# A one-core decoder block on Trainium2: turns placed later among the MLP's matmuls, first rows' passes ahead of a turn, decay buffers apart, and the gate chain in another order

## What is computed

```python
x = x + attn(layernorm(x))        # a Mamba-2 mixer, then a gated MLP (width 1024)
x = x + xattn(layernorm(x), ctx)  # an mLSTM cell: q from x, k = v = ctx, 4 heads of 64
x = x + ffn(layernorm(x))         # FP4 quantised gate/up/down, width 704

# gates of the cell: i and f are linear in [q, k, v]
lf = log_sigmoid(f); cs = cumsum(lf)
log_D[s, t] = cs[s] - cs[t] + lf[t] + i[t]   for t <= s
m = rowmax(log_D); D = exp(log_D - m)
C = (q k^T / 8) * D
h = C / (max(|rowsum(C)|, exp(-m)) + 1e-8) @ v      # then a per-head norm
```

## Time and profile before

| | |
|---|---|
| median of 3 runs | 634.5 us (633.87 to 637.78) |
| the profiled execution | 634.09 us, of which 632.3 us are the profile's span |
| PE busy | 575.8 us, 91% |
| DVE busy | 446.1 us, 71% |
| ACT busy | 270.2 us, 43% |
| POOL busy | 145.6 us, 23% |
| mean granted TensorE clock | 0.959 of 2.4 GHz |

### The profile page before, as it was taken

The page is one execution under the profiler, slowest core; times in us unless marked ns, Lnnn a source line. Parts: engine busy times, 40 slices in busy tenths (PEclk is TensorE's granted clock), DMA queues, the critical chain, the costliest instruction groups (busy, mean ns, idle before and its releaser), DMA issues. The chain is left out here.

```text
span 632.3 us, 9628 instructions
## 1 busy us (share of the span) xinstructions
PE 575.8 (91%) x3023; PEld 467.0 (74%) x3023; DVE 446.1 (71%) x969; ACT 270.2 (43%) x563; POOL 145.6 (23%) x209
## 2 busy tenths in 40 slices
PE   7799998999999889899999999679975899999995
PEld 6576665788888778777888888668862577777774
DVE  5885898299896134444445456657898999999994
ACT  3566777776794421221111110155523344444431
POOL 4120000145543110111011010203575322222200
PEclk9899998799999989999999999799976899999998
DMA  8201001000000500000000000223400000000000
GB/s 296 91 18 33 17 13 55 4 23 6 6 4 2 202 2 1 1 1 1 0 1 1 1 1 0 68 71 110 142 17 1 1 10 16 17 17 17 17 18 25
DMA packets 22528, 20.99 MB, mean 33 GB/s; under 512 B 12120, under 2 KB 20696, under 8 KB 22104
## 3 DMA queue, kind: packets, MB, share of 16 engines
q1 hardware_dynamic: 22008, 20.41, 10.0%
q10 hardware_dynamic: 480, 0.07, 0.1%
HBM read 16.04 MB, written 2.34 MB: 29 GB/s over the span
## 5 line engine op out<-in xcount | busy, mean ns | idle before, releaser
L762 PE MATMUL ps<-xnT,w_fc 128*128 128x256 f32 x512 | 113.9, 383 | 0.0
L762 PEld LDWEIGHTS ps<-xnT,w_fc 128*128 128x128 f32 x512 | 97.5, 192 | 13.1
L1545 PE MATMUL ps<-w_fc,scores 128*128 128x352 f32 x256 | 83.0, 479 | 6.1 <-ACT scores L1611 6.1
L1545 PEld LDWEIGHTS ps<-w_fc,scores 128*128 128x128 f32 x256 | 49.1, 197 | 33.9 <-ACT scores L1611 8.2
L1165 DVE TENSOR_TENSOR xs<-ps,xs 128x512 f32<-128x512 f32 x32 | 22.1, 692 | 71.3 <-ACT xs L972 71.3
L972 ACT ACTIVATE xs<-ps 128x512 f32<-128x512 f32 x32 | 19.1, 597 | 104.9 <-PE ps L762 67.2
L775 PE MATMUL ps<-zs,xs 128*128 128x256 f32 x256 | 56.6, 379 | 0.0
L775 PEld LDWEIGHTS ps<-zs,xs 128*128 128x128 f32 x256 | 48.6, 190 | 6.6
L1060 DVE SCALAR_TENSOR_TENSOR fold<-xpad,conv_w,fold 128x256 f32<-128x256 f32 x120 | 50.6, 479 | 0.8
L1563 PE MATMUL ps<-u_res,hT 128*128 128x256 f32 x192 | 45.9, 391 | 3.8 <-DVE scores L1717 2.8
L1563 PEld LDWEIGHTS ps<-u_res,hT 128*128 128x128 f32 x192 | 37.4, 195 | 11.8 <-issue 3.0
(11 more groups left out here) (266 smaller groups left out, 1185.2 us busy)
## 6 DMA issues: line engine op xcount, KB each, us to landing
zs<-in_ffn_w SPq DMA_DIRECT2D x1, 2112.0 KB, 10.7
x_res<-in_x SPq DMA_DIRECT2D x8, 256.0 KB, 7.4
w_fc<-in_w_fc SPq DMA_DIRECT2D x1, 2048.0 KB, 10.3
xnT<-in_ctxT SPq DMA_DIRECT2D x8, 256.0 KB, 3.1
xs<-in_ctxT SPq DMA_DIRECT2D x8, 256.0 KB, 3.3
xs<-xnT SPq DMA_DIRECT2D x8, 256.0 KB, 3.4
xs<-in_ctx SPq DMA_DIRECT2D x16, 128.0 KB, 2.6
out<-scores SPq DMA_DIRECT2D x16, 128.0 KB, 1.7
```

Source lines behind the costliest of these rows:

```text
L762: last = pe.matmul(bank[half + r][:, i * S:(i + 1) * S], m.w_fc1[:, kk, col:col + P], m.xnT[:, b, kk * S:(kk + 1) * S], start=(kk == 0), s ...
L1545: last = pe.matmul(bank[1 + j][:, 0:HALF], xT[:, p, k * P:(k + 1) * P], m.w_gu[:, k, j * HALF:(j + 1) * HALF], start=(k == 0), stop=(k == ...
```

## The change

- **MLP** (steps 18 on): PE does `turn_xn(b-5)` after pair 2 of `fc1` instead of before it; ACT does `turned_xn` at the end of the same step instead of at the start of the next.
- **First rows**: in step 3, PE does both passes `rows(0, 0)` and `rows(0, 1)` before `turn_u(4)`, instead of after it and near the step's end.
- **Decay buffers apart**: `segs` keeps only `stationary` and `moving`; the working buffers lie in `e_own` and in the last batch's part of `xs`. `set_segs` goes; three DVE memsets (as 1024 float32 a partition each) stand at the very start, before `stats(0)`. SP waits for its own store of the rows. `rmax` lies in the `stationary` half of `segs` afterwards and is cleared by POOL in step 19 (`fills`), with the ones for the scan.
- **Gate chain**: `gate_rows` writes the gate values in the layout the chain wants, so the four copies go; `lf + i` is formed before the turn; the scan and the operation after it read PSUM itself; the parts of R come before `nm`. PE turns six weight groups first, then 4 `keep_warm` transposes instead of 26, then `lf`, then `lf + i`, then the other six groups; the last 10 `keep_warm` go. ACT stores the parts after all saves, then does the exp of `nm`. POOL sets only the ones column of `v`. ACT ends front with a small Exp.

```diff
@@ -208,6 +208,8 @@
...
         m.graw = sb("graw", [P, T, 2 * XH])
+        m.gates = sb("gates", [P, 2, C, B * XH])
+        m.run_ones = sb("run_ones", [B * XH, S])
         m.a_tok = sb("a_tok", [P, C * B * XH])
...
@@ -235,6 +237,8 @@
...
             m.scores = sb("scores", [P, B, 3 * P])
+            m.segs = sb("segs", [P, 2048])
+            m.rmax = m.segs[:, 0:1024].bitcast(BF16).rearrange("p (r t) -> p r t", r=2)
             m.dt = sb("dt", [P, T, NH])
...
@@ -433,19 +437,22 @@
     W = T * NH
-    segs = sb("segs", [P, 2048])
-    over_segs = carver(segs)
-    work = [over_segs(f"sp{k}", [P, W]) for k in range(5)]
-    raw = over_segs("dt_raw", [P, W])
-    ones = over_segs("ones", [P, P])
-    both = over_segs("cs", [P, 2, P])
-    rest = over_segs("cs_rest", [P, 2, P])
-    pieces = over_segs("cs_pieces", [P, 3 * P]).bitcast(BF16).rearrange("p (g k t) -> p g k t", g=2, k=3)
+    segs = m.segs
+    over_e = carver(e_own)
+    work = [over_e(f"sp{k}", [P, W]) for k in range(5)]
+    raw = over_e("dt_raw", [P, W])
+    ones = over_e("ones", [P, P])
+    over_last_x = carver(m.xs[:, T - C:, :].rearrange("p t e -> p (t e)"))
+    both = over_last_x("cs", [P, 2, P])
+    rest = over_last_x("cs_rest", [P, 2, P])
+    pieces = over_last_x("cs_pieces", [P, 3 * P]).bitcast(BF16).rearrange("p (g k t) -> p g k t", g=2, k=3)
     rows_dram = nc.dram_tensor("segment_rows", (W, 6, P), BF16).ap()
...
     ROWS_IN = 4 * 16
+    PAIR_OF_ONES = 1.0 + 0x3F80 * 2.0 ** -23
+    PAIR_OF_MINUS_ONES = -(1.0 + 0xBF80 * 2.0 ** -23)
     CTX_SUMS = B - 1
...
@@ -503,6 +510,7 @@
...
         sp.dma_start(rows_dram, pieces.rearrange("p g k t -> p (g k) t")).then_inc(s["seg_stored"], 16)
+        sp.wait_ge(s["seg_stored"], 16)
         sp.wait_ge(s["segs_set"], 1)
...
@@ -589,9 +597,17 @@
...
+        def fills():
+            pool.wait_ge(s["seg_ps"], 2 * T)
+            pool.memset(m.rmax, 0.0)
+            pool.memset(m.run_ones[:], 1.0).then_inc(s["filled"], 1)
+            pool.wait_ge(s["filled"], 2)
+
         for k in range(STEPS):
...
             on(rstds, 2 * k + 1)
+            if k == MLP + 1:
+                fills()
             if k == 4:
...
@@ -803,8 +819,12 @@
...
                 on(channels, k - 2, [0, 1, 2])
+                if k == 3:
+                    rows(0, 0)
+                    rows(0, 1)
                 on(turn_u, 2 * k - 2)
-                on(rows, k - 3, 0)
+                if k > 3:
+                    on(rows, k - 3, 0)
                 on(channels, k - 2, [3, 4])
...
@@ -812,7 +832,8 @@
...
                     sum_steps()
-                on(rows, k - 3, 1)
+                if k > 3:
+                    on(rows, k - 3, 1)
                 on(turn_x, k - 3, 1)
...
@@ -838,8 +859,11 @@
...
                 ctx_sums_last()
-            on(turn_xn, b - 5)
+            if k < MLP:
+                on(turn_xn, b - 5)
             on(fc1, k - MLP, 2)
+            if k >= MLP:
+                on(turn_xn, b - 5)
             on(fc1, k - MLP, 3)
...
@@ -979,7 +1003,8 @@
...
                 step_exp()
-            on(turned_xn, b - 6)
+            if k <= MLP:
+                on(turned_xn, b - 6)
             for i in range(3):
...
@@ -1011,11 +1036,18 @@
...
             on(silu_gate, k - MLP, 3)
+            if k >= MLP:
+                on(turned_xn, b - 5)
             on(turned_q, k - MLP - 2)
+        act.activation(ve[:, 0, :], m.minus_half[:, 0:C], ACT.Exp)
...
         dve.memset(xpad[:, :, :, 0:PAD], 0.0).then_inc(s["pads_clear"], 1)
+        dve.memset(segs[:, 0:1024], 0.0)
+        dve.memset(segs[:, 1024:2048], PAIR_OF_MINUS_ONES).then_inc(s["segs_kept"], 1)
+        dve.wait_ge(s["segs_kept"], 1)
+        dve.memset(segs[0:12, 0:1024], PAIR_OF_ONES).then_inc(s["segs_set"], 1)
...
@@ -1100,13 +1132,6 @@
...
-        def set_segs():
-            dve.wait_ge(s["seg_stored"], 16)
-            dve.memset(stationary, 0.0)
-            dve.memset(moving, -1.0).then_inc(s["segs_kept"], 1)
-            dve.wait_ge(s["segs_kept"], 1)
-            dve.memset(stationary[0:12, :, :], 1.0).then_inc(s["segs_set"], 1)
-
         def inputs(b):
...
@@ -1185,8 +1210,9 @@
...
             here = m.graw[:, C * b:C * (b + 1), :]
-            dve.tensor_tensor(here, bank[7][:, 0:C * 2 * XH].rearrange("p (c g) -> p c g", c=C),
-                              here, ALU.add).then_inc(g["gates_saved"], 1)
+            dve.tensor_tensor(m.gates[:, :, :, XH * b:XH * (b + 1)],
+                              bank[7][:, 0:C * 2 * XH].rearrange("p (c g h) -> p g c h", c=C, g=2),
+                              here.rearrange("p c (g h) -> p g c h", g=2), ALU.add).then_inc(g["gates_saved"], 1)
...
@@ -1219,8 +1245,6 @@
...
                 soft_rest()
-            if k == 8:
-                set_segs()
             on(convolve, k - 2, [2, 3])
...
@@ -1255,13 +1279,12 @@
...
     rest = sb("max_rest", [ROWS, 2, S])
-    ig = sb("ig", [P, C, ROWS])
-    fg = sb("fg", [P, C, ROWS])
+    ig, fg = (m.gates[:, k].rearrange("p c r -> p (c r)") for k in range(2))
+    shifted = sb("ig_lf", [P, C * ROWS])
     lf = sb("lf", [P, C * ROWS])
     work = [sb(f"lsp{k}", [P, C * ROWS]) for k in range(5)]
-    igT, lfT, cs, aT, R, nm = (sb(n, [ROWS, S]) for n in ("igT", "lfT", "cs", "aT", "R", "nm"))
-    ones = sb("ones", [ROWS, S])
-    s = m.plain("gt_dve gt_act gt_pe gt_ones w_turned w_saved")
+    cs, aT, R, nm = (sb(n, [ROWS, S]) for n in ("cs", "aT", "R", "nm"))
+    s = m.plain("gt_dve gt_act gt_pe gt_pad w_turned w_saved")
...
@@ -1277,26 +1300,21 @@
...
     BETWEEN = 6
-    by_chunk = lambda lo: m.graw[:, :, lo:lo + XH].rearrange("p (b c) h -> p c b h", c=C)
-    split = lambda t: t[:].rearrange("p c (b h) -> p c b h", h=XH)
     block = m.block
...
     def _(pool):
-        pool.memset(m.w_dn[FF - (KF - 1) * P:, KF - 1, :], 0.0).then_inc(s["gt_ones"], 1)
-        pool.wait_ge(s["gt_ones"], 1)
-        pool.memset(ones[:], 1.0).then_inc(s["gt_ones"], 1)
+        pool.memset(m.w_dn[FF - (KF - 1) * P:, KF - 1, :], 0.0).then_inc(s["gt_pad"], 1)
+        pool.wait_ge(s["gt_pad"], 1)
...
     def _(dve):
-        for c in range(C):
-            dve.tensor_copy(split(fg)[:, c], by_chunk(XH)[:, c])
-            last = dve.tensor_copy(split(ig)[:, c], by_chunk(0)[:, c])
-        last.then_inc(s["gt_dve"], 1)
-        dve.wait_ge(s["gt_dve"], 1)
-        softplus_start(dve, s["gt_dve"], fg[:].rearrange("p c r -> p (c r)"), work, -1.0)
-        n = softplus_finish(dve, s["gt_dve"], s["gt_act"], lf[:], work, -1.0, 3)
+        softplus_start(dve, s["gt_dve"], fg, work, -1.0)
+        n = softplus_finish(dve, s["gt_dve"], s["gt_act"], lf[:], work, -1.0)
+        dve.wait_ge(s["gt_dve"], n)
         m.lf_at = n
+        dve.tensor_tensor(shifted[:], ig, lf[:], ALU.add).then_inc(s["gt_dve"], 1)
+        n += 1
...
@@ -1305,24 +1323,23 @@
...
         dve.wait_ge(s["gt_pe"], 1)
-        dve.tensor_copy(igT[:], bank[0][0:ROWS, 0:S])
-        step(dve.tensor_copy(lfT[:], bank[1][0:ROWS, 0:S]))
-        dve.wait_ge(s["gt_ones"], 2)
-        step(dve.tensor_tensor_scan(cs[:], ones[:], lfT[:], 0.0, ALU.mult, ALU.add))
-        step(dve.scalar_tensor_tensor(aT[:], cs[:], -1.0, lfT[:], ALU.mult, ALU.add))
-        step(dve.tensor_tensor(aT[:], aT[:], igT[:], ALU.add))
+        step(dve.tensor_tensor_scan(cs[:], m.run_ones[:], bank[1][0:ROWS, 0:S], 0.0, ALU.mult, ALU.add))
+        dve.wait_ge(s["gt_pe"], 2)
+        step(dve.scalar_tensor_tensor(aT[:], cs[:], -1.0, bank[0][0:ROWS, 0:S], ALU.mult, ALU.add))
+        m.a_at = n
         step(dve.tensor_tensor_scan(R[:], aT[:], aT[:], -3e38, ALU.max, ALU.max))
-        step(dve.tensor_tensor(nm[:], cs[:], R[:], ALU.add))
-        m.nm_at = n
         step(dve.tensor_copy(parts[:, 0, :], R[:]))
...
         m.parts_at = n
+        step(dve.tensor_tensor(nm[:], cs[:], R[:], ALU.add))
+        m.nm_at = n
         dve.tensor_scalar(m.out_w[:], m.out_w[:], 1.0, None, ALU.add)
-        dve.wait_ge(s["gt_pe"], 2)
+        dve.wait_ge(s["gt_pe"], 3)
         dve.tensor_copy(m.a_tok[:], bank[2][:, 0:C * ROWS])
+        dve.wait_ge(s["gt_pe"], 4)
         dve.tensor_scalar(m.nm_tok[:], bank[3][:, 0:C * ROWS], 1e-8, None, ALU.add).then_inc(m.gates_done, 1)
...
@@ -1335,24 +1352,15 @@
...
-        for n in range(BETWEEN):
+        for n in range(len(groups)):
             save(n)
+        act.wait_ge(s["gt_dve"], m.parts_at)
+        act.dma_start(m.rows_dram, parts[:]).then_inc(m.max_stored, 16)
         act.wait_ge(s["gt_dve"], m.nm_at)
         act.activation(nm[:], nm[:], ACT.Exp, scale=-1.0).then_inc(s["gt_act"], 1)
-        act.wait_ge(s["gt_dve"], m.parts_at)
-        act.dma_start(m.rows_dram, parts[:]).then_inc(m.max_stored, 16)
-        for n in range(BETWEEN, len(groups)):
-            save(n)
...
     def _(pe):
-        keep_warm(pe, m, 26)
-        pe.wait_ge(s["gt_dve"], m.lf_at)
-        for c in range(C):
-            pe.transpose(bank[0][0:ROWS, c * P:(c + 1) * P], ig[:, c, :], m.ident[:])
```

(28 more changed lines are left out.)

## The result

| | before | after |
|---|---|---|
| median of 5 runs each | 634.64 us (633.87 to 637.78) | 621.24 us (616.92 to 623.39) |
| ratio of the times | | 0.9767, 95% interval 0.9738 to 0.9796 |
| the profiled execution | 634.09 us | 616.92 us, of which 615.2 us are the span |
| PE busy | 575.8 us | 568.1 us |
| mean granted TensorE clock | 0.959 | 0.961 |

The profiled execution came out at 616.92 us against the 617.3 forecast for it, and the median at 621.24 against 617.7.

A forecast was written before the change was run, and what follows sets the result against it. TensorE was taken to set the pace in front, DVE's chain with the store and load of R in the gate chain; 9.7 + 2.1 + 2.9 + 2.1 = 16.8 us off 634.09 gave 617.3, median 617.7, range 611.5 to 625.5.

The forecast's parts named there:

- part 1: MLP, turns behind pair 2: 6.5 us of waits, 1.5 before gates, 1.7 of slow clock, sum 9.7 us.
- part 3: Step 9, set_segs gone from DVE: wait 1.3 us shorter, rows pass 1.6 us faster, gain 2.9 us.
- part 4: Gate chain: store issued 3.8 us earlier, 1.7 us lost to slow clock behind it, net 2.1 us.
- The slack of 1 us: MLP: pair 2 takes 3.5 us, longest wait 2.5 us, so the turn comes 1 us after normed is done.
- rival (b): MLP: the wait only moves to ahead of pair 3, 6.5 and 1.7 us stay; 625.9 us, chance 0.12.
- Part 2: First rows passes ahead in step 3: PE 4.2 us ahead, then meets DVE at turn_u(6), 36.25; gain 2.1 us.
- The memsets at the start: Start, DVE: three of 0.91 us, 2.7 us from about 1 us, done by 3.7 before stats(0); no cost.
- the clock's price: Gate chain: 5 us of tiny transposes bring half clock; args and first scores lose 1.7 us, bounds 0 and 3.4.
- rival (a): Gate chain: the clock holds over the gap, 16.8 + 1.7 us gained; 616.0 us, chance 0.25.
- the prediction's own sign of being wrong: Front ends less than 12 us earlier, or PE's clock is low in the cell for more than one batch.
- rival (d): Cell: TensorE enters at half clock and stays there, 4.9 us a batch, +39 over eight; 655 us, chance 0.03.
- Rival (c): Front, steps 4 to 10: ACT catches the gains, parts 2 and 3 give nothing; 622.7 us, chance 0.12.

The follow-up runs named there:

- turn_back: The changed kernel with turn_xn and turned_xn back where they were in the MLP; 629.99 us, ratio 0.9922 to before.
- after_again: The changed kernel itself, run again for its spread and a second profile (after's second trace, 620.78 us); median 619.35 us, ratio 0.9753 to before.
- fill_turn: The changed kernel with 20 idle transposes ahead of turn_u(6) in step 4; 621.29 us, ratio 0.9768 to before.
- gates_back: The changed kernel with gate chain, its memsets, copies and idle transposes as before, no small Exp ending front; 619.42 us, ratio 0.9764 to before.
- warm: The changed kernel with 24 idle transposes between the turns of aT and nm and 18 behind nm's; 616.45 us, ratio 0.9704 to before.
- warm_half: The changed kernel with only the 24 idle transposes between the turns of aT and nm, without the last 18; 618.29 us, ratio 0.9748 to before.
- rows_more: The changed kernel with one more rows pass, rows(1, 0), ahead of turn_u(6) in step 4; 619.76 us, ratio 0.9758 to before.

## Why the prediction was right, and where it was off

In the trace the parts gave 17.1 us for the 16.8 forecast. That they come so close is partly luck: part 1 gave 0.8 us more than its sum and part 3's stretch 1.6 more, part 4 gave 2.0 less. The median stands 4.3 us above the profiled execution, so it missed its forecast by 3.5 us.

**Part 1**, 9.7 us forecast, 10.5 in the trace and 10.6 by undoing it. Its sum stood on three rows, 6.5 of wait, 1.5 before `gates`, 1.7 of slow clock, and turn_back returned each: 6.5, 1.5 and 8.76 - 7.07 = 1.7. The slack of 1 us was enough; rival (b), a wait that only moves, has no wait in after's trace to its name. The remaining 0.8 us can be placed by the starts. Where nothing waits, a group starts 0.16 us before the modelled end of the one ahead (in after 227.08 + 3.62 is 230.70, and the next starts at 230.54); a wait takes this overlap too, so four waits cost 0.6 us beyond their own length. And behind a wait the first group is longer at full clock, 0.66 for 0.60 us in two turns and 1.03 for 0.96 in `gates`: 0.2 us.

**Part 2**, 2.1 us forecast, 2.1 at `turn_u(6)`. The reasoning, that PE would be 4.2 us ahead and would then stand before DVE, is what happened: 36.33 for 36.25. The step it left out is what a wait there does. The prediction said that PE "then meets DVE" and gave the meeting no price, while its paragraph on part 4 counted three of four waits of such length with half clock behind them. In one trace of after the clock held, in the other it did not, 1.7 us. The runs give the part 1.0 to 1.8 us, which their intervals don't separate from nothing.

**Part 3**, 2.9 us forecast, 3.1 to the decay matrices and 1.4 behind them. Both terms were right: 1.42 us of the wait gone (1.3), and 1.69 us for the warm pass (1.6). Most of the 1.4 us behind it was not the change's: the rows pass at 105.15 is the warm one, but in after's second trace the same pass took 3.10 us, as before's 3.13. Between the decay matrices and `fc1` before took 95.91 us, after 94.54 and after's second trace 95.87: it was the luck of the profiled run. Undoing part 3 gives 3.3 us.

The memsets at the start were forecast at 2.7 us, done by 3.7, at no cost. Each took 0.91 us, as the one of the earlier trace rows, the first two while POOL was busy with its memsets and masks, so POOL didn't keep DVE off; the rule of the Trainium skill, page "SBUF — State Buffer", section "Who interferes with whom", agrees with these rows. But the end is 4.29, not 3.7: the first starts at 1.12, and between them lie 0.17 and 0.27 us. `stats(0)` starts at 4.22 for 3.91 and the first turn at 7.14 for 6.92, 0.2 us. The three durations were added and the gaps between them left out.

**Part 4**, 3.8 - 1.7 = 2.1 us forecast, 4.0 - 3.9 = 0.1 in the trace, and nothing that can be told by undoing it. The gain was sized well, step by step: `lf` done at 389.30, 4.3 us after the chain's start (forecast 4.4); PE later by 0.65 us with its `lf` turn; 394.07 for the store, 9.1 us in (9.4). The two operations that now read PSUM take 0.68 and 0.41 us. The first took 0.68 out of SBUF too. The second is just what its SBUF neighbour L1337 takes, 0.41, so no 0.13 us shows, which the page "VectorE: DVE Perf Modes" of the Trainium skill, section on the TRN2 errata, would add; for this size the row decides.

The step that failed is the clock's price. The forecast was right that the clock would fall (rival (a), that it holds, did not come in any trace with the changed chain and its waits unfilled) and said "it stayed there some 3.5 us, twice the 1.7 us that it cost". That length was taken from the MLP, where PE had dense matmuls at once behind its one wait. Here a wait of 2.83 us, two tiny transposes, 1.95 us more of wait and one instruction of `args` come first, and then the clock was low from 397 to past 406 us, 9 us for 3.5 (the window of 406 to 408 us has 0.90): both `args`, all of the first `scores` and more. Its cost, 3.9 us, lies outside even the bound of 3.4, and the prediction's own sign of being wrong, a low clock in the cell for more than one batch, came. Its count of waits was off too: before's trace has a fifth wait of this length, which brought nothing, so three of five brought half clock and not three of four:

```profile
397.79 0.66 PE L785 MATMUL ps<-ident,xs 128*128 128x128 f32 x4 [2.73 <-DVE xs L1201]
```

The clock didn't stay low for good: the batches from the second on stand 6.0 and 6.6 us apart in after as in before, so rival (d) did not come.

**Rival (c)**, that ACT catches what front gains, was wrong in the trace of after: 2.1, 3.1 and 1.4 us all arrive at `fc1`, 6.5 us.

**The median.** The sum was made against one execution, and 0.4 us was added for the median, which was what before showed. After's five runs spread over 6.5 us (616.92 to 623.39), before's five over 3.9; but the thirteen runs of before in the first set spread over 5.4 (633.13 to 638.56, mean clock 0.949 to 0.960), so most of such a spread was there before the change. The granted clock goes roughly with the time: in after's five runs it is 0.961 at 616.92, 0.950 at 620.59, 0.953 at 621.24 and 621.84, and 0.947 at 623.39; in the first set of experiments it is 0.961 again at 617.08 and 0.948 at 623.58.

The two traces of after, 616.92 and 620.78 us, show where one execution loses against another. By the marks of the table the second is behind by 0.3 us at `turn_u(6)`, 2.0 at the decay matrices, 3.3 at `fc1`, 4.5 at the chain's start, 4.1 at `args`, and 3.9 at `den` and at the end. The steps of 1.7, 1.3 and 1.2 us lie at three falls of the clock: the rows pass behind `turn_u(6)` (1.88 and 2.78 us), the one behind the gate sums (1.94 and 3.10), and the last `turn_q` with the `gates` behind it (0.66 and 0.96 us, and 1.12 and 1.72). From the second trace's timeline:

```profile
107.27 3.10 PE L668 MATMUL ps<-fold,xnT 128*128 128x512 f32 x4
...
384.06 1.12 PE L801 MATMUL ps<-ident,xs 128*128 128x128 f32 x4 [2.72 <-DVE xs L1227]
```

Behind `den` the two take the same time, so the overlap of cell and FFN, the rival in after_again's text, has no part in this difference. As far as two traces can show it, the 3.5 us by which the median missed are falls of the clock that come in some executions and not in others, and the profile caught an execution with few of them. Only one of the three places, the wait of 2.43 us before `turn_u(6)`, was made by the change. How many places there are in all is open: fill_turn took one away and its median didn't move, and the other runs have no trace.

## What to carry to other kernels

Price a gap on TensorE twice: its own length, and the slow matmuls behind it, which here cost 1.7 us in a dense stretch and 3.9 in one broken by further waits. When idle transposes are taken out because the work beside them got shorter, look at what waits remain there: in the trace, 24 and 18 of them won back all that the cell had lost behind the shorter gate chain. And make the forecast of a median from more than the one profiled execution where its runs differ in their mean clock.

## What the runs showed of the hardware

The same wait on TensorE, in the same code, can leave its clock at 1.00 or bring it to 0.50. Behind 2.42 to 2.43 us before `turn_u(6)` the rows pass was warm in three traces (1.88 us in after, turn_back and gates_back) and slow in two (2.78 in after's second, 3.11 in warm); behind 2.15 us there it was slow too (2.95 in warm_half). Behind 2.72 to 2.73 us before the last `turn_q` the turn took 0.66 us in four traces (before, after, warm_half, rows_more) and 1.11 to 1.12 in the eight others that have this wait. Behind the waits of 0.7 to 1.4 us shown above the work was warm; behind those of 4.25 us it was slow in both traces that have one.

The clock also falls with no wait in front: to 0.50 in fill_turn behind sixteen matmuls of 8 columns at 54 us, with PE busy for at least 1.98 us of every 2 from 38 us on. The rows pass behind 24 such matmuls (the context's gate sums) took 1.94 us in four of the thirteen traces and 2.93 to 3.61 in the nine others, and by the next `turn_x`, behind 32 more, every one of the thirteen was at half clock (1.11 to 1.12 us for 0.60). That the narrow matmuls are the cause is argued from where the falls lie; no run widened them.

A DVE operation of 128x64 took 2.77 us with POOL's memsets of 1.79 and 0.95 us beside it and 0.19 without (they weren't tried alone), while two of DVE's own memsets of 1024 words, beside POOL's small memsets and mask work, stayed at the 0.91 us of the earlier trace rows.
